# Ones-matmuls among the first transposes, a 17-column v row, and a reordered last stage in a channel-attention + MoE kernel

## The reference

```python
x = x + _L0_conv_ref(_gn(x), w_qkv, w_dw, w_proj, temperature)
x = x + _L1_conv_ref(_gn(x), gate_w, gate_b, w1, b1, w2, b2)
# L0: qkv = 1x1 conv (288x96), then a depthwise 3x3 conv;
#     q, k are l2-normalised per channel; scores = q k^T per head (8 heads of 12 channels, over 256 pixels)
#     out = proj(softmax(scores * temperature) v)
# L1: scores = softmax(x_flat @ gate_w + gate_b); top 2 of 4 experts
#     coef[e] = sum over the two ranks r of (expert e was chosen as rank r by ANY token) * weight_r(token)
#     out = sum_e coef[e] * (w2[e] relu(w1[e] x + b1[e]) + b2[e])
```

## Time and profile before

| | us |
|---|---|
| median of 3 runs (lowest, highest) | 178.86 (178.29, 179.58) |
| the profiled execution: its own time | 179.8 |
| span of that execution | 178.0 |
| busy PE / DVE / ACT / POOL | 156.8 / 143.0 / 109.7 / 59.0 |

### The profile page before, as it was taken

The page is one execution under the profiler, slowest core; times in us unless marked ns, Lnnn a source line. Parts: engine busy times, 40 slices in busy tenths (PEclk is TensorE's granted clock), DMA queues, the critical chain, the costliest instruction groups (busy, mean ns, idle before and its releaser), DMA issues.

```text
span 178.0 us, 3567 instructions
## 1 busy us (share of the span) xinstructions
PE 156.8 (88%) x1259; PEld 123.8 (70%) x1259; DVE 143.0 (80%) x386; ACT 109.7 (62%) x248; POOL 59.0 (33%) x74
## 2 busy tenths in 40 slices
PE   0599999999999989996999999989967797679973
PEld 0589999999999979996999998856722332123332
DVE  2894895879999999999949889678554389899993
ACT  2590297649393770980855638756847496889740
POOL 6130222515143225323227224604450005163630
PEclk9999999999999999998589999999996999999999
DMA  5603483320404013040005000000000000111312
GB/s 138 153 0 84 108 228 104 101 54 18 134 0 136 17 43 109 2 129 24 2 0 153 4 4 0 0 2 4 0 0 0 0 0 0 44 44 44 90 49 88
DMA packets 9370, 9.39 MB, mean 53 GB/s; under 512 B 3720, under 2 KB 8168, under 8 KB 9352
## 3 DMA queue, kind: packets, MB, share of 16 engines
q1 hardware_dynamic: 9208, 8.92, 18.4%
q10 hardware_dynamic: 144, 0.24, 0.4%
HBM read 2.28 MB, written 1.57 MB: 22 GB/s over the span
## 4 chain that ended last, share of the span: by engine, by line
PE 47%; DVE 36%; ACT 6%; issue 5%; DMA 4%; DVEq 0%
DVE v_acc L1314 12%; PE qk_ps L859 6%; PE qk_ps L861 6%; DVE h_mixed L1585 4%; DVE stats L1268 3%; PE v_ps L1141 3%; PE v_ps L906 2%; DMA x_sb<-in_x 2%; PE mix_ps L1141 2%; PE out_ps L956 2%; PE qk_ps L848 2%; PE qk_ps L850 2%; PE qk_ps L849 2%; PE qk_ps L864 2%; DMA out<-xs 2%
## 5 line engine op out<-in xcount | busy, mean ns | idle before, releaser
L1314 DVE SCALAR_TENSOR_TENSOR v_acc<-v_ps,v_taps,v_acc 96x576 f32<-96x576 f32 x64 | 51.9, 811 | 7.3 <-ACT v_acc L483 6.1
L859 PE MATMUL qk_ps<-w_a,x_a 128*128 128x192 f16 x261 | 52.6, 253 | 0.0
L861 PE MATMUL qk_ps<-w_b,x_b 128*128 128x192 f16 x261 | 52.4, 253 | 0.0
L859 PEld LDWEIGHTS qk_ps<-w_a,x_a 128*128 128x128 f16 x261 | 27.3, 105 | 0.7 <-issue 0.3
L861 PEld LDWEIGHTS qk_ps<-w_b,x_b 128*128 128x128 f16 x261 | 26.3, 101 | 0.5
L864 PE MATMUL qk_ps<-w_c,x_c 96*128 96x192 f16 x87 | 22.1, 255 | 0.0
L795 POOL TENSOR_TENSOR x_sb<-x_sb,xn 96x512 f32<-96x512 f32 x8 | 12.4, 1558 | 28.5 <-ACT xn L593 28.5
L1585 DVE TENSOR_TENSOR h_mixed<-h_mixed,hidden 128x512 f32<-128x512 f32 x24 | 20.3, 884 | 1.2 <-ACT h_mixed L615 1.2
L756 POOL TENSOR_TENSOR sq_sum<-qk_sq 128x384 f32<-128x384 f32 x8 | 8.0, 999 | 32.6 <-ACT qk_sq L500 29.2
L559 ACT ACTIVATE sc_exp<-sc_qk,neg_max 96x12 f32<-96x12 f32 x16 | 4.7, 296 | 20.5 <-DVE neg_max L1353 20.5
L765 POOL TENSOR_TENSOR rstd<-var_eps,minus_half 96x2 f32<-96x2 f32 (+2 forms) x9 | 8.5, 942 | 21.1 <-DVE var_eps L1294 21.1
(11 more groups left out here) (223 smaller groups left out, 380.2 us busy)
## 6 DMA issues: line engine op xcount, KB each, us to landing
x_b<-x_a SPq DMA_DIRECT2D x7, 324.0 KB, 3.1
x_sb<-in_x SPq DMA_DIRECT2D x8, 192.0 KB, 3.9
out<-xs SPq DMA_DIRECT2D x7, 192.0 KB, 2.1
x_a<-x_lo SPq DMA_DIRECT2D x7, 108.0 KB, 2.5
x_b<-x_lo SPq DMA_DIRECT2D x7, 108.0 KB, 2.4
x_c<-x_lo SPq DMA_DIRECT2D x21, 36.0 KB, 1.9
w_sb<-in_L_conv_w SPq DMA_DIRECT2D x2, 144.0 KB
cst<-in_consts ACTq DMA_DIRECT2D x1, 236.0 KB, 3.8
```

Source lines behind the costliest of these rows:

```text
L859: eng.matmul(to, window(x_a[p][:, dx, b], half, dy), w_a[:, t, :], start=(t == 0), stop=False, skip_group_check=True)
L861: mm = eng.matmul(to, window(x_b[p][:, dx, b], half, dy), w_b[:, t, :], start=False, stop=False, skip_group_check=True)
L1314: eng.scalar_tensor_tensor(out=v_acc[i % 3][:, :, :], in0=v_window(dy, dx), scalar=v_taps[:, t:t + 1], in1=v_acc[i % 3][:, :, :], op0=ALU. ...
```

## The change

Five edits, as a diff with the line numbers of both files left out of the argument:

```diff
-VP = W + 2
+VP = W + 1
-RELU_DVE = (18, 20, 22)
+RELU_DVE = (8, 9, 18, 20, 22)
@@ v_window, project_v
-            at = (1 + dy) * VP + 2 + dx
+            at = (1 + dy) * VP + 1 + dx
-  to = v_bank[b][0:C, VP:VP + VLEN].rearrange("c (h w) -> c h w", w=VP)[:, :, 2:VP]
+  to = v_bank[b][0:C, VP:VP + VLEN].rearrange("c (h w) -> c h w", w=VP)[:, :, 1:VP]
@@ scalar
             normalise2(7)
+            top_exps(0)
             high_xn2(6)
-            relu(8)
-            relu(9)
+            relu(10)
             high_xn2(7)
-            top_exps(0)
-            relu(10)
             gate_exps(1)
...
+            bias_tile(0)
             coefs(1)
-            bias_tile(0)
             bias_tile(1)
-            top_exps(1)
             for i in range(2, PAIRS):
+                if i == 3:
+                    top_exps(1)
@@ gpsimd
-            sum_squares(7)
@@ tensor
-            keep_warm(2)
+            keep_warm(4, qk_ps[1])
             eng.wait_ge(wc_set, 1)
             turn_taps(0, 3)
+            keep_warm(1, qk_ps[1])
             prepare_v()
+            keep_warm(2, qk_ps[1])
             eng.wait_ge(wc_set, 2)
             turn_taps(3, 6)
             eng.wait_ge(wc_last, 3)
-            turn_taps(6, TAPS)
+            turn_taps(6, 8)
+            keep_warm(1, qk_ps[1])
+            turn_taps(8, TAPS)
             project_v(0, (0,))
...
+                if i == 0:
+                    keep_warm(4, mix_ps)
                 if i + 1 < PAIRS:
                     project_v(i + 1)
...
             gram(7)
+            norms(7, 48)
             gate(2, 7, 0, 24)
+            mix_heads(6)
             first(1)
-            norms(7, 48)
-            mix_heads(6)
...
             first(4)
+            apply_mix(7)
             norm_means(7, 3)
-            apply_mix(7)
             norm_vars(7)
@@ vector
+            def sum_squares_last():
+                sq = qk_sq[:, :, :].rearrange("p (b h) o -> p b h o", b=2)
+                eng.wait_ge(qk_taken, 2 * PAIRS)
+                eng.wait_ge(sq_ready, PAIRS - 1)
+                eng.tensor_tensor(sq_sum[:, :, :], sq[:, :, 0, :], sq[:, :, 1, :], ALU.add).then_inc(sq_ready, 1)
...
+            sum_squares_last()
             head_attn(6)
...
             channel_means(7)
-            add_dev(7)
             gate_compare(0)
             add_mix(7)
-            add_eps(7)
             x1_stats(7)
             channel_means(8)
+            add_dev(7)
+            gate_rank(0)
+            add_eps(7)
+            gate_present(0)
             make_shift(7)
+            add_dev(8)
             take_logits(4)
-            add_dev(8)
-            gate_rank(0)
-            gate_present(0)
             add_eps(8)
+            make_shift(8)
             gate_scores(0)
-            make_shift(8)
-            gate_weights(0)
-            gate_split(0)
+            relu(8)
+            relu(9)
             take_logits(5, 3)
             gate_logits(1)
+            gate_weights(0)
             gate_compare(1)
             gate_rank(1)
             gate_present(1)
-            relu(18)
+            gate_split(0)
...
             eng.tensor_reduce(slope[:, :, :], slope_own[:, :, :, :], AX.X, ALU.add).then_inc(slope_ready, 1)
+            relu(18)
             relu(20)
```

## The result

| | us |
|---|---|
| before, median of 4 runs (lowest, highest) | 179.22 (178.29, 180.65) |
| changed, median of 4 runs (lowest, highest) | 186.21 (183.94, 186.78) |
| ratio changed/before, 95% interval | 1.034 (1.021 to 1.047) |
| profiled execution of the changed kernel: its own time, span | 186.26, 184.5 |
| mean granted clock of the profiled executions, before and changed | 0.971, 0.898 |

The forecast was 174.9, with a range of 171.5 to 179.0.

What follows compares the result with a forecast made beforehand. Bound by TensorE at low clock at the start, TensorE and DVE in the main loop, then TensorE, with a ring of waits late and DVE full at the end; +0.7 - 1.2 - 3.5 = -4.0 from 178.9 gave 174.9 us, range 171.5 to 179.0.

Steps and rivals of the forecast that it cites:

- The new wait at `norm_vars(7)` brings the clock down: Rival, last stage: TensorE's wait for add_dev(7) lowers its clock, costing half of 3.4 us, total 176.6; chance 0.12.
- the bounds of the last stage: Limits on the last stage's -3.5 us: 0 if the new wait costs the level, -5.2 if norm_vars(7) does not wait.
- the work around it is dense: Argument at norm_vars(7) against a clock fall after the 1.7 us wait; that rival's total was 176.6, chance 0.12.
- The start: Up to project_v(1): ones-matmuls raise TensorE's clock at about 12 us, but packs land later; +0.7 us, between -0.7 and +4.0.
- the four calls: Ones-matmul calls before project_v(1), forecast at 0.25 us each; 2.0 us together at the low or 1.0 at the high level.
- it takes the dense 128-row products: At the start: 96-row products did not raise TensorE's clock; 128-row products from 22.59 did, about three microseconds later.
- Taps: DVE's tap instructions on 17-column v rows: 37 ns shorter each, 33 counting between about 34 and 82 us; -1.2 us.
- So the low stretch after it stays: Pair 5: the 1.45 us TensorE wait hardly shrinks, so the 6.9 us low-clock stretch, costing 3.4 us, remains.
- the first rival: The low-clock stretch after pair 5 goes too, giving 3.4 us more, total 171.5; chance 0.12.
- The last pair's squares and `spread_rk(7)`: Last pair: addition moved from POOL to DVE; TensorE waits 0.3 us for it, spread_rk(7) moves to 115.8; +0.3 us.
- The new order: Last stage: reordered instructions remove the 2.37 us wait before first(15) and the second clock dip; -3.5 us, the +0.3 included.
- the sum -4.0: Whole kernel: +0.7 at the start, -1.2 for shorter taps, -3.5 in the last stage; median 174.9 us.

Runs made afterwards that it cites:

- e4: The changed kernel with the start of before: two ones-matmul calls before the first transposes, none elsewhere; median 182.18 us.
- e7: The kernel before with only add_dev(7) and add_eps(7) moved behind channel_means(8) on DVE; median 182.52 us, ratio 1.033.
- e8: The changed kernel with twelve ones-matmul calls in TensorE's wait for pair 0's packs, without the four before project_v(1); median 183.77 us, ratio 1.038.
- e2: The changed kernel with six ones-matmuls between norm_means(7) and norm_vars(7), filling that wait; median 177.29 us, ratio 0.990.
- e1: The changed kernel with add_dev(7) and add_eps(7) put back in their old places on DVE; median 175.64 us, ratio 1.007.
- e5: The changed kernel with add_dev(7) and add_eps(7) in old places, ones-matmuls in five TensorE waits, none before project_v(1); median 175.12 us, ratio 0.972.
- e9: The changed kernel with add_dev(7) and add_eps(7) in old places, TensorE's long waits filled with ones-matmuls, including before second(2) and eight before turn_u(1); median 174.53 us.
- e11: The kernel before with five ones-matmuls before pair 5's spread_rk(4) and nine before first(15), nothing of the change; median 173.74 us.
- e3: The kernel before with only the v rows changed to 17 columns; median 177.82 us.
- e6: The kernel before with only the start's edits: eight ones-matmuls among the first transposes, four before project_v(1); median 182.90 us, ratio 1.034.
- e10: The changed kernel with add_dev(7), add_eps(7) and the start as before, later TensorE waits filled with ones-matmuls, none at the packs; median 171.03 us.

## Why the prediction was wrong, step by step

**The step that failed: "The new wait at `norm_vars(7)` brings the clock down", left out of the sum.** The wait itself was forecast at 1.7 us, and came at 1.63. Its effect on the clock stood among the rivals with a chance of 0.12 and a price of half of 3.4 us; the bounds of the last stage allowed it 3.5. The four profiled executions with this wait (1.62 to 1.89 us: changed, e4, e7, e8) all fell behind it, and e2 puts the price at 10.8 us in the last stage. Chance and price were both far too small. Against it I had put that "the work around it is dense". TensorE was indeed busy 20.3 of 20.3 us, and the clock stayed at 1.2 GHz. I had copied the price from the dip after pair 5, 6.9 us long. Here the low level lasted 20.3 us, through four gates (eight records of small float32 matmuls each) and the `first` between them, to 3.9 us behind the last gate. In e1's profiled execution it also ended about 4 us behind the last gate. That the gates are why it lasted so long is not shown: no run takes them out or moves them. The right price would have been half the length of the stretch at 1.2 GHz, and nothing in the profile of before told that length. What it did show is a fall behind a wait of 1.45 us and one of 2.37, and none behind 1.55 us at 154.0 (clock 1.00 from 154.0 to 157.2). A new wait between these in length deserved a large chance. The wait of 1.55 us, in TensorE's timeline and windows of before:

```profile
154.00 1.93 PE L1141 MATMUL mix_ps<-h_mixed,w2T 128*96 128x512 f32 x4 [1.55 <-DVE h_mixed L1585]
...
154.00:157.20 3.20, 2.02 (x5) 0.62 (x5) 3.03 (x9) 3.20 (x6) 1.26 (x1) 1.00 0.10 33
```

**The start, +0.7 forecast, +2.56 found.** Most of its mechanism held: the level rose at about 12 us (the products at 13.23 are 0.085 us apart, against 0.16), TensorE idled 3.60 us (about 3 forecast) until 23.09 (22.3), and fell. Two terms were mis-sized. The packs came 0.8 us later than forecast, and the 42 products took 6.08 us instead of 4.94; the four calls took 0.92. The 4.94 came from an execution in which TensorE had not idled before the packed products; here the stretch begins after a fall (clock 0.56 over 6.1 us). The early rise bought nothing because the packs, not TensorE, set the start. Even with the wait filled (e5, e8, e9) `project_v(1)` comes at 26.57 to 27.80, where the six profiled executions with the start of before have it at 25.00 to 27.55. For that start does not rise at a fixed time: the steps become 0.083 us at about 25 us in four of the six, but at 17.2 in e7 and at 16.2 in e11, both during products on 96 rows. So my reading that it takes the dense 128-row products was wrong. In all seven profiled executions with the new start the steps are short from the first product on, so the ones-matmuls go with an early rise every time; they are not its only cause.

**Taps, -1.2 forecast, -1.08 found.** 37 ns were forecast for each, and 811 - 777 = 34 found. What they give hangs on the start, though. e3, whose `project_v(1)` comes at 27.55 as before, reaches pair 5's `spread_rk(4)` at 81.34 instead of 81.92, only 0.58 sooner. With `project_v(1)` at about 30.1 it is 1.08 (changed kernel, 53.31 us on, against e6, 54.39).

**"So the low stretch after it stays."** It did not: -3.05 us. The wait there went from 1.45 to 1.25 us, as forecast ("hardly shrinks"), but the clock stayed up (window 83.4 to 108.3: 1.00). That was the first rival, at 0.12. But the length of the wait does not decide it. These are the profiled executions in which it was not filled:

| wait (us) | run: stretch from `spread_rk(4)` to `first(0)` |
|---|---|
| 1.45 | before 27.98, e6 27.98, e7 24.95 |
| 1.25 or 1.26 | changed 24.93, e1 24.92, e2 24.93, e8 24.92, e3 26.44, e4 26.44 |

24.9 us is the stretch at full clock (24.92 to 24.94 where it was filled), 26.44 goes with a low stretch of about 3 us, 27.98 with one of over 6. So the gain of 3.05 us was at least in part luck of the profiled execution; how much of it is the change, nine executions don't tell. What decides whether the clock falls there is open.

**The last pair's squares and `spread_rk(7)`, +0.3.** Seen from `first(0)` it moved from 5.55 to 5.86 us.

**The new order, -3.5.** Most of its steps were right: 0.51 us before `first(22)` (0.7 forecast), the one before `first(20)` still 0.93. The one before `first(15)` is gone in the changed kernel, where TensorE runs late at half clock; at full clock 0.38 us of it are left in e2 and 0.68 in e10. e2 is the kernel of the forecast with the clock left alone there, and from `first(0)` to the end it takes 65.4 us instead of 68.1: -2.7, against -3.5 forecast. Both orders at full clock differ by 2.5 us (e10 against e11); there the old order has lost its dip as well, which the forecast counted as a gain of the new one.

So the sum -4.0 became +6.5, by what each part came out above its forecast: +1.9 at the start, +0.1 for the taps, -3.05 at pair 5 and +11.6 in the last stage. Of these 11.6, e2 gives back 10.8 with six matmuls into a bank that nobody reads.

## What to carry to other kernels

When a change makes TensorE wait somewhere new, ask what stands behind the wait, and how long it would run at half clock: a wait of 1.6 us cost about 9 us here, because TensorE then worked for 20 us at 1.2 GHz. Fill such a wait with matmuls on constants into a free bank, about as long as the wait; that took the changed kernel from 186.2 to 177.3 and the kernel before, with two waits filled, from 177.0 to 173.7. And compare several executions with their mean clocks before a gain of a per cent is believed or given up: the time at full clock tells what an order is worth, and how often the clock is lost is a second question. Two profiles of different kernels, one with a fall and one without, do not show that the edit made the difference.

## What the runs showed of the hardware that was not expected

- A TensorE without a gap stayed at 1.2 GHz for 20.3 us (changed kernel), with gates of eight 96-column float32 records among 512-column products. It rose 3.9 us after the last gate.
- The length of an idle time does not tell whether the level falls. 1.62 to 1.89 us was followed by a fall in all four profiled executions, but 1.55 (before, at 154.0) was not. In pair 5, 1.45 was in two of three and 1.25 or 1.26 in two of six. Twice a fall followed two short ones: 0.52 and 0.89 (e1), 0.93 and 0.51 (changed); e2 has 0.94 and 0.51 without a fall.
- At the start the granted clock reads full while the steps are those of 1.2 GHz; only the distances between starts tell the level there, and when it rises differs between executions of one start (16.2, 17.2 and about 25 us).
- The kernel before alone covers 173.2 to 180.7 us. Its four executions at a mean clock of 1.00 took 173.2 to 174.0, those at 0.952 took 180.1 to 180.4. In between the clock is a rough guide: 175.6 to 178.4 at 0.99, 176.4 to 178.3 at 0.98, 177.0 to 177.8 at 0.961, but 179.8 and 180.0 at 0.971.
